# One stage of a fused image network: row sums from a ones column, a first key tile weighed in fp32, and one VectorE copy fewer

## The chip, the cores and the metric

The kernel runs on one core of a Trainium2 chip, in one launch. The metric is the device time of the whole launch in microseconds (us), the median of several runs. Only one of the kernel's stages is changed, and that stage takes about a sixth of the time.

## The reference, cut to what matters

The network has a windowed attention block, a gated convolution-like block, a plain self-attention, a pooling mixture of experts, a second attention with query, key and value weights, and a routed mixture of experts. It works on 32 images of 1024 tokens with 64 channels. The changed stage is the plain self-attention on layer-normed tokens:

```python
def _L2_attn_ref(seq):
    attn = jnp.einsum('blc,bmc->blm', seq, seq)
    attn = jax.nn.softmax(attn, axis=2)
    out = jnp.einsum('blm,bmc->blc', attn, seq)
    return out
...
t = t + _L2_attn_ref(_ln_t(t))        # t: 32 x 1024 x 64, fp32
```

Queries, keys and values are all the same normed tokens z. For one image the scores are z z^T (1024 x 1024), the weights are their softmax, and the result is the weights times z.

## The kernel before

The stage is `stage_attend`. Tokens stay on chip in fp32: 128 partitions by 8 tiles of 64 channels per image. Products keep fp32 accuracy by splitting each operand into a high f16 part and a low f16 rest. Since the score matrix is symmetric, a tile of 128 keys by 1024 queries that TensorE makes can be used as the stationary operand of the weighing directly, without a transpose.

An image has NT = 8 key tiles. For tile m the work is:

- **scores** (PE, L1259 and L1260): four matmuls of 512 columns into one of two PSUM buffers `ps_s`, from `xT` (high and low parts over each other) and from `xTb`, the same with its halves swapped by a DMA (L1140);
- **exp** (ACT, L1213): `ex` = exp(score - 55) in fp32, in a ring of 4, with the row sum taken by the instruction's accumulator into `rs`, which is a second instruction, ACTIVATION_READ_ACCUMULATOR;
- **high part** `exh` in f16: on ACT (L1219) for five tiles, on DVE (L1173) for tiles 1, 4 and 7;
- **low part** `exl` = `ex` - `exh` in f16 (DVE, L1166);
- **weighing** (PE, L1274 to L1277), LAG = 4 tiles later: for each of 8 query tiles three matmuls of 64 columns, high x high, high x low and low x high, summed in PSUM over all 8 key tiles. Each parity h of images has a bank of its own in `ps_o`.

After an image's last key tile DVE takes the reciprocal of the row sums (L1178), scales the result (L1181) and adds it to the tokens (L1184). These three are called the finish below.

The next images are prepared between the tiles by the slots `near` (next image) and `far` (next but one): at far 0 DVE sums and centres (L69, L74); at far 2 ACT squares (L80) and DVE reduces the squares (L85); at far 3 POOL makes the reciprocal root (L90, L92) and at far 4 the normed tokens `xn` (L98); at near 2 ACT takes their high part (`cut_high`, L106) and POOL the low part (`cut_low`, L113); at near 4 PE turns them (L126) into `ps_t` and DVE copies that to `xT` (L136), after which SP issues the two DMAs that fill `xTb`.

The order on each engine is written out by `stream` (L1047): for m = 0 to 7 it calls `step(m)` and the near and far slots. PE is given near and far after its step, as ACT and POOL are; DVE has `near_first`. In DVE's step m come the low part of tile m - 1, then its high part of tile m if it has one, then the finish, which was placed at step 4 of the next image. In PE's step m come the scores of tile m, then the weighing of the tile 4 back.

The waits that tie the engines: scores of tile m wait for exp of tile m - 2 (`exped`); exp of tile m waits for the low part of tile m - 4 (`low`); a weighing waits for its low part; scores of tile 0 wait for the DMAs (`swapped`). `cut_high` of the next image waits on ACT until the image before the current one has been weighed to its last tile (L1197), since it writes over that image's `hl`.

## Time and profile before

| what | value |
|---|---|
| median of 3 runs | 3016.01 us (3010.62 to 3026.71) |
| the profiled execution's own time | 3013.47 us |
| its span | 3011.3 us |
| mean granted TensorE clock | 0.923 of full speed |
| busy over the span: PE, DVE, ACT, POOL | 76%, 77%, 71%, 58% |

The changed stage lies between about 957 and 1489 us of the span. The shares above are means over all stages, so the stage has to be looked at by itself. An instruction's busy time and the time to the start of the next on its engine differ by up to 0.1 us, since instructions overlap at their ends; sums of a sequence therefore go by the distance between starts.

### The profile page before, as it was taken

What the parts mean: (1) busy time and instruction counts of PE and PEld (TensorE: products, weight loads), DVE (VectorE), ACT (ScalarE), POOL (GpSimd) and SP (SyncE); (2) the same over time, 40 slices, a digit from 0 to 9 for tenths busy, and PEclk for the clock granted to TensorE, in tenths of its full rate; (3) what the DMA queues carried; (4) which work ended last, traced back from release to release, by engine and by line L of the source; (5) the groups of instructions that cost most, each with busy time, mean ns of one, the idle gap of its engine ahead of it and who ended that gap; (6) DMA issues with size and microseconds to landing.
All of it is one profiled execution on the core that took longest, in us unless ns stands there. A gap on an engine that the chain in (4) does not pass through costs nothing. (4 is left out here: it accounts for less than half of the span.)

```text
span 3011.3 us, 86006 instructions
## 1 busy us (share of the span) xinstructions
PE 2282.4 (76%) x33244; PEld 1642.6 (55%) x33244; DVE 2327.7 (77%) x3714; ACT 2132.5 (71%) x3776; POOL 1742.0 (58%) x1370
## 2 busy tenths in 40 slices
PE   3777777778774888888644585888888888777777
PEld 1555555555552655555433473776777676545444
DVE  3677778777774999999867325888888887688897
ACT  2677777777773999999722112888888887777776
POOL 3577777777764333333266202998999898733331
PEclk9999999999996999999957556999999999899999
DMA  3211111111100000000000200000000000000101
GB/s 72 49 44 42 36 37 39 42 42 31 27 16 4 18 17 14 17 17 15 12 1 1 52 5 2 9 5 5 6 7 5 5 7 7 4 22 21 24 21 25
DMA packets 144669, 62.22 MB, mean 21 GB/s; under 512 B 118676, under 2 KB 127798, under 8 KB 144566
## 3 DMA queue, kind: packets, MB, share of 16 engines
q1 hardware_dynamic: 139565, 58.00, 9.0%
q10 hardware_dynamic: 4393, 2.77, 0.4%
q8 instruction: 73, 1.20, 0.2%
q14 instruction: 30, 0.25, 0.0%
q0 software_dynamic: 608, 0.01, 0.0%
HBM read 14.50 MB, written 8.39 MB: 8 GB/s over the span
## 5 line engine op out<-in xcount | busy, mean ns | idle before, releaser
L1813 POOL TENSOR_TENSOR a_prl<-a_pr,a_prh 128x1024 f16<-128x1024 f32 x256 | 544.9, 2142 | 47.8 <-ACT a_prh L1790 46.1
L1730 DVE TENSOR_REDUCE a_nmax<-a_ps_a 128x1 f16<-128x1024 f32 x256 | 312.2, 1219 | 34.0 <-PE a_ps_a L1852 32.1
L1166 DVE TENSOR_TENSOR a_exl<-a_ex,a_exh 128x1024 f16<-128x1024 f32 x256 | 319.4, 1269 | 8.4 <-ACT a_exh L1219 6.2
L1213 ACT ACTIVATE a_ex<-a_ps_s,a_shift 128x1024 f32<-128x1024 f32 x256 | 281.5, 1101 | 21.1 <-DVE a_exl L1166 12.8
L1790 ACT ACTIVATE a_prh<-a_pr 128x1024 f16<-128x1024 f32 x256 | 270.6, 1057 | 8.1
L1868 PE MATMUL a_ps_s<-a_qx,a_kh 128*128 128x128 f16 x2048 | 259.1, 220 | 2.7 <-issue 2.6
L1786 ACT ACTIVATE a_pr<-a_ps_s 128x1024 f32<-128x1024 f32 x256 | 259.5, 1014 | 0.0
L1870 PE MATMUL a_ps_s<-a_qm,a_kl 128*128 128x128 f16 x2048 | 259.2, 220 | 0.0
L2115 ACT ACTIVATE f_mixed_s<-f_ps_e,f_gates 128x64 f32<-128x64 f32 x1024 | 212.7, 426 | 40.1 <-PE f_ps_e L395 37.2
L113 POOL TENSOR_TENSOR a_w_hl<-a_w_xn,a_w_hl 128x512 f16<-128x512 f32 (+1 forms) x64 | 82.4, 1288 | 273.2 <-ACT a_w_hl L106 273.2
L1274 PEld LDWEIGHTS a_ps_o<-a_w_hl,a_exh 128*128 128x128 f16 x2048 | 181.9, 98 | 91.2 <-DVE a_exl L1166 66.2
L1274 PE MATMUL a_ps_o<-a_w_hl,a_exh 128*128 128x64 f16 x2048 | 207.1, 194 | 25.8 <-DVE a_exl L1166 25.8
L1868 PEld LDWEIGHTS a_ps_s<-a_qx,a_kh 128*128 128x128 f16 x2048 | 201.9, 99 | 34.7 <-issue 5.9
L1884 PE MATMUL a_ps_o<-a_vh,a_prh 128*128 128x65 f16 x2048 | 217.8, 196 | 3.3 <-POOL a_prl L1813 3.2
L1259 PE MATMUL a_ps_s<-a_w_xT 128*128 128x512 f16 x512 | 196.5, 384 | 31.0 <-DMA a_xTb<-a_w_xT 26.9
L1886 PE MATMUL a_ps_o<-a_vl,a_prh 128*128 128x65 f16 x2048 | 218.2, 193 | 0.0
L1870 PEld LDWEIGHTS a_ps_s<-a_qm,a_kl 128*128 128x128 f16 x2048 | 201.9, 99 | 29.5 <-issue 0.6
L1888 PE MATMUL a_ps_o<-a_vh,a_prl 128*128 128x65 f16 x2048 | 217.1, 194 | 0.0
L1852 PE MATMUL a_ps_a<-a_kh,a_qx 128*128 128x512 f16 x512 | 156.6, 388 | 68.0 <-DVE a_nmax L1730 63.5
L1277 PE MATMUL a_ps_o<-a_w_hl,a_exl 128*128 128x64 f16 x2048 | 206.2, 193 | 0.0
L1276 PE MATMUL a_ps_o<-a_w_hl,a_exh 128*128 128x64 f16 x2048 | 206.2, 193 | 0.0
L90 POOL TENSOR_TENSOR f_w_var<-f_w_ss,eps 128x8 f32<-128x8 f32 x64 | 12.8, 200 | 317.6 <-DVE f_w_ss L85 317.6
(344 smaller groups left out, 8526.7 us busy)
## 6 DMA issues: line engine op xcount, KB each, us to landing
tokens<-in_x_dram SPq DMA_DIRECT2D x32, 256.0 KB, 2.9
bl_qg<-bl_qk_high SPq DMA_DIRECT2D x128, 64.0 KB, 2.0
bl_km<-bl_qk_high SPq DMA_DIRECT2D x256, 32.0 KB, 2.0
a_xTb<-a_w_xT SPq DMA_DIRECT2D x64, 128.0 KB
out_dram<-tokens SPq DMA_DIRECT2D x32, 256.0 KB, 2.6
bl_qg<-bl_qk_low SPq DMA_DIRECT2D x64, 64.0 KB, 2.0
bl_km<-bl_qk_low SPq DMA_DIRECT2D x128, 32.0 KB, 2.0
a_qm<-a_qx SPq DMA_DIRECT2D x64, 64.0 KB, 2.0
```

What stands on the lines that cost most here:

```text
L1166: nc.vector.tensor_tensor(exl[:, at[2]], ex[:, r], exh[:, at[2]], ALU.subtract).then_inc(low, 1)
L1213: nc.scalar.activation(ex[:, r], ps_s[:, m % 2], ACT.Exp, bias=shift[:], accum_out=rs[at[1]][:, m:m + 1]).then_inc(exped, 1)
L1274: nc.tensor.matmul(out, e_high, z_high, start=(k == 0 and g == 0), stop=False, skip_group_check=True)
L1730: nc.vector.tensor_reduce(nmax[:, g:g + 1], ps_a[:], AX.X, ALU.max, negate=True).then_inc(maxed, 1)
L1786: nc.scalar.activation(pr[:, r], ps_s[:, m % 2], ACT.Exp).then_inc(exped, 1)
L1790: nc.scalar.activation(prh[:, r], pr[:, r], ACT.Copy).then_inc(high, 1)
L1813: nc.gpsimd.tensor_tensor(prl[:, r], pr[:, r], prh[:, r], ALU.subtract).then_inc(low, 1)
L1868: nc.tensor.matmul(out, kh[ha][:, keys], qx[ha][:, queries], start=True, stop=False, skip_group_check=True)
L1870: last = nc.tensor.matmul(out, kl[ha][:, keys], qm[ha][:, queries], start=False, stop=True, skip_group_check=True)
L1884: nc.tensor.matmul(out, high_j, vh[ha][:, j], start=(j == 0), stop=False, skip_group_check=True)
L1886: nc.tensor.matmul(out, high_j, vl[ha][:, j], start=False, stop=False, skip_group_check=True)
L1888: last = nc.tensor.matmul(out, low_j, vh[ha][:, j], start=False, stop=(j == NT - 1), skip_group_check=True)
```

## The change

- **Row sums.** The exp loses its accumulator output. `hl` is laid out as low, high, ones: the high part moves to columns 64 to 127 and column 128 holds 1.0. The two matmuls of a weighing that have the high part of z as moving operand take 65 columns, so the last column of each query tile's result is its row sum. The reciprocal reads that column from PSUM.
- **Three shared banks.** A result is now 8 x 65 = 520 columns, more than a bank's 512. The two parities lie in three banks: one from column 57 to 577, one from 959 to 1479. In the middle bank the first has its query tile 7, the second its query tile 0.
- **First key tile in fp32.** The exp of tile 0 goes to a buffer of its own, `whole`, and has no high and no low part: PE weighs it in fp32 against `xn` with a ones column (`xn1`), 8 matmuls of 65 columns in place of 24. Seven of them are issued in that tile's place, the eighth (the one in the shared bank) ahead of tile 1's weighing, after a wait for the scaling of the image before (`normed`).
- **High parts.** DVE takes those of tiles 2 and 5 in place of 1, 4 and 7. ACT has five as before.
- **Order on DVE.** The finish moves from the end of step 4 to the start of step 3, and now waits for the last weighing before the reciprocal.
- **POOL.** `xn` of the next image but one is made at far 6 in place of far 4, after a wait for the current image's tile 1 to be weighed, since PE reads `xn1`.

```diff
--- before.py
+++ after.py
@@ -100,17 +100,19 @@
-def cut_high(nc, ln, n1, w, x, n=C):
+def cut_high(nc, ln, n1, w, x, n=C, high=0):
     nc.scalar.wait_ge(ln["normed"], n1)
-    nc.scalar.activation(w["hl"][:, :, 0:n], x[:, :, 0:n], ACT.Identity).then_inc(ln["high"], 1)
-def cut_low(nc, ln, n1, w, x, engine=None, n=C):
+    nc.scalar.activation(w["hl"][:, :, high:high + n], x[:, :, 0:n], ACT.Identity).then_inc(ln["high"], 1)
+def cut_low(nc, ln, n1, w, x, engine=None, n=C, high=0):
...
     engine.wait_ge(ln["high"], n1)
-    engine.tensor_tensor(w["hl"][:, :, C:C + n], x[:, :, 0:n], w["hl"][:, :, 0:n], ALU.subtract).then_inc(ln["pair"], 1)
+    low = C - high
+    engine.tensor_tensor(w["hl"][:, :, low:low + n], x[:, :, 0:n], w["hl"][:, :, high:high + n],
+                         ALU.subtract).then_inc(ln["pair"], 1)
@@ -1080,25 +1082,29 @@
...
     RING, PARTS, LAG = 4, 8, 4
-    VECTOR_HIGH = (1, 4, 7)
+    WHOLE = 0
+    VECTOR_HIGH = (2, 5)
     with ExitStack() as ctx:
...
-        wk = [work_buffers(sb, f"w{h}") for h in range(2)]
+        wk = [work_buffers(sb, f"w{h}", ("sum", "ss", "var", "rstd", "xc", "sq", "hl", "xT")) for h in range(2)]
         xTb = [sb(f"xTb{h}", [P, TOK], F16) for h in range(2)]
...
         exl = sb("exl", [P, PARTS, TOK], F16)
-        rs = [sb(f"rs{h}", [P, NT], F32) for h in range(2)]
+        whole = sb("whole", [P, TOK], F32)
+        xn1 = [sb(f"xn1{h}", [P, NT, C + 1], F32) for h in range(2)]
+        for h in range(2):
+            wk[h]["xn"] = xn1[h][:, :, 0:C]
         rinv = [sb(f"rinv{h}", [P, NT], F32) for h in range(2)]
...
         ps_s = ctx.enter_context(nc.psum_tensor("a2_ps_s", [P, 2, TOK], F32))
-        ps_o = ctx.enter_context(nc.psum_tensor("a2_ps_o", [P, 2, 512], F32))
+        ps_o = ctx.enter_context(nc.psum_tensor("a2_ps_o", [P, 3 * 512], F32))
         ps_t = ctx.enter_context(nc.psum_tensor("a2_ps_t", [P, TOK], F16))
         ln = net.norms[0]
-        swapped, shift_set = (sem("a2_" + s) for s in ("swapped", "shift_set"))
+        swapped, shift_set, ones_set = (sem("a2_" + s) for s in ("swapped", "shift_set", "ones_set"))
@@ -1107,10 +1113,19 @@
...
+        OUTS = (512 - 7 * (C + 1), 1024 - (C + 1))
+        outs = [tiles(ps_o[:, at:at + NT * (C + 1)]) for at in OUTS]
+        SHARED, FRESH = (7, 0), ((0, 7), (0, 1))
         def count(at, lag=0):
...
             return NT * (2 * i + h) + m - lag + 1
+        def low_count(at):
+            i, h, m = at
+            return (NT - 1) * (2 * i + h) + m
@@ -1118,7 +1133,11 @@
...
                 return high_v, len(VECTOR_HIGH) * (2 * i + h) + before
-            return high_s, (NT - len(VECTOR_HIGH)) * (2 * i + h) + m + 1 - before
+            return high_s, (NT - 1 - len(VECTOR_HIGH)) * (2 * i + h) + m - before
+        def exps(at):
+            return whole[:] if at[2] == WHOLE else ex[:, at[2] % RING]
@@ -1143,6 +1162,9 @@
...
                 nc.vector.memset(shift[:], -SHIFT2).then_inc(shift_set, 1)
+                for h in range(2):
+                    nc.vector.memset(wk[h]["hl"][:, :, 2 * C:2 * C + 1], 1.0).then_inc(ones_set, 1)
+                    nc.vector.memset(xn1[h][:, :, C:C + 1], 1.0).then_inc(ones_set, 1)
@@ -1159,31 +1181,29 @@
...
                 def step(i, h, m):
+                    at = tile_at(i, h, m - LAG)
+                    if at and m == LAG - 1 or at and m == NT + LAG - 1:
+                        ia, ha, _ = at
+                        n = 2 * ia + ha
+                        dve.wait_ge(weighed, count(at))
+                        nc.vector.reciprocal(rinv[ha][:], outs[ha][:, :, C]).then_inc(inverted, 1)
+                        dve.wait_ge(inverted, n + 1)
+                        nc.vector.tensor_tensor(o[ha][:], outs[ha][:, :, 0:C], spread(rinv[ha][:], C),
+                                                ALU.mult).then_inc(normed, 1)
+                        dve.wait_ge(normed, n + 1)
+                        nc.vector.tensor_tensor(tv[:, ia, ha], tv[:, ia, ha], o[ha][:], ALU.add).then_inc(added, 1)
                     at = tile_at(i, h, m - 1)
-                    if at:
-                        r = at[2] % RING
+                    if at and at[2] != WHOLE:
                         dve.wait_ge(*high_count(at))
-                        nc.vector.tensor_tensor(exl[:, at[2]], ex[:, r], exh[:, at[2]], ALU.subtract).then_inc(low, 1)
+                        nc.vector.tensor_tensor(exl[:, at[2]], exps(at), exh[:, at[2]], ALU.subtract).then_inc(low, 1)
                     at = now(i, h, m)
                     if at and at[2] in VECTOR_HIGH:
-                        r = at[2] % RING
                         dve.wait_ge(exped, count(at))
...
                             dve.wait_ge(weighed, count(at, PARTS))
-                        nc.vector.tensor_copy(exh[:, at[2]], ex[:, r]).then_inc(high_v, 1)
-                    at = tile_at(i, h, m - LAG - 1)
-                    if at and at[2] == NT - 1:
-                        ia, ha, g = at
-                        n = 2 * ia + ha
-                        nc.vector.reciprocal(rinv[ha][:], rs[ha][:]).then_inc(inverted, 1)
-                        dve.wait_ge(inverted, n + 1)
-                        dve.wait_ge(weighed, count(at))
-                        nc.vector.tensor_tensor(o[ha][:], tiles(ps_o[:, ha]), spread(rinv[ha][:], C),
-                                                ALU.mult).then_inc(normed, 1)
-                        dve.wait_ge(normed, n + 1)
-                        nc.vector.tensor_tensor(tv[:, ia, ha], tv[:, ia, ha], o[ha][:], ALU.add).then_inc(added, 1)
-                stream(dve, step, near, far, LAG + 1, near_first=True)
+                        nc.vector.tensor_copy(exh[:, at[2]], exps(at)).then_inc(high_v, 1)
+                stream(dve, step, near, far, LAG, near_first=True)
                 dve.wait_ge(added, B)
@@ -1195,7 +1215,7 @@
...
                             act.wait_ge(weighed, NT * (2 * i + h - 1))
-                        cut_high(nc, ln, n + 1, w, w["xn"])
+                        cut_high(nc, ln, n + 1, w, w["xn"], high=C)
@@ -1204,19 +1224,18 @@
...
                     if at:
-                        r = at[2] % RING
                         act.wait_ge(scored, count(at))
-                        if past(at, RING):
-                            act.wait_ge(low, count(at, RING))
-                        if at[2] == 0 and past(at, 2 * NT):
-                            act.wait_ge(added, 2 * at[0] + at[1] - 1)
-                        nc.scalar.activation(ex[:, r], ps_s[:, m % 2], ACT.Exp, bias=shift[:],
-                                             accum_out=rs[at[1]][:, m:m + 1]).then_inc(exped, 1)
-                        if at[2] not in VECTOR_HIGH:
+                        if at[2] == WHOLE:
+                            if past(at, NT - 1):
+                                act.wait_ge(weighed, count(at, NT - 1))
+                        elif past(at, RING) and at[2] - RING != WHOLE:
+                            act.wait_ge(low, low_count(tile_at(at[0], at[1], at[2] - RING)))
+                        nc.scalar.activation(exps(at), ps_s[:, m % 2], ACT.Exp, bias=shift[:]).then_inc(exped, 1)
+                        if at[2] != WHOLE and at[2] not in VECTOR_HIGH:
                             act.wait_ge(exped, count(at))
...
                                 act.wait_ge(weighed, count(at, PARTS))
-                            nc.scalar.activation(exh[:, at[2]], ex[:, r], ACT.Copy).then_inc(high_s, 1)
+                            nc.scalar.activation(exh[:, at[2]], exps(at), ACT.Copy).then_inc(high_s, 1)
@@ -1225,13 +1244,15 @@
...
                     if k == 2:
-                        cut_low(nc, ln, n + 1, w, w["xn"], nc.gpsimd)
+                        cut_low(nc, ln, n + 1, w, w["xn"], nc.gpsimd, high=C)
...
                         norm_rstd(nc, ln, n + 1, w, net.nhalf[:], net.eps[:])
-                    if k == 4:
+                    if k == 6:
+                        if not isinstance(i, int) or 2 * i + h >= 2:
+                            pool.wait_ge(weighed, NT * (2 * i + h - 2) + WHOLE + 2)
                         norm_apply(nc, ln, n + 1, w, nc.gpsimd)
@@ -1262,22 +1283,38 @@
...
                         ia, ha, k = at
-                        pe.wait_ge(low, count(at))
-                        if k == 0 and past(at, 2 * NT):
-                            pe.wait_ge(added, 2 * ia + ha - 1)
-                        z_high, z_low = wk[ha]["hl"][:, k, 0:C], wk[ha]["hl"][:, k, C:2 * C]
+                        if k == WHOLE:
+                            pe.wait_ge(exped, count(at))
+                        else:
+                            pe.wait_ge(low, low_count(at))
+                        z_high, z_low = wk[ha]["hl"][:, k, C:2 * C + 1], wk[ha]["hl"][:, k, 0:C]
+                        def weigh_whole(g):
+                            return nc.tensor.matmul(outs[ha][:, g], whole[:, P * g:P * g + P], xn1[ha][:, WHOLE],
+                                                    start=g in FRESH[ha], stop=False, skip_group_check=True)
+                        if k == WHOLE:
+                            for g in range(NT):
+                                if g != SHARED[ha]:
+                                    ins = weigh_whole(g)
+                            ins.then_inc(weighed, 1)
+                            return
+                        if k == WHOLE + 1:
+                            if past(at, NT):
+                                pe.wait_ge(normed, 2 * ia + ha)
+                            weigh_whole(SHARED[ha])
                         for g in range(NT):
-                            out = ps_o[:, ha, C * g:C * g + C]
+                            out = outs[ha][:, g]
                             e_high = exh[:, k, P * g:P * g + P]
...
-                            nc.tensor.matmul(out, e_high, z_high, start=(k == 0 and g == 0), stop=False,
+                            nc.tensor.matmul(out, e_high, z_high, start=False, stop=False, skip_group_check=True)
+                            nc.tensor.matmul(out[:, 0:C], e_high, z_low, start=False, stop=False,
                                              skip_group_check=True)
-                            nc.tensor.matmul(out, e_high, z_low, start=False, stop=False, skip_group_check=True)
                             ins = nc.tensor.matmul(out, e_low, z_high, start=False, stop=(k == NT - 1),
...
+                pe.wait_ge(ones_set, 4)
                 stream(pe, step, near, nothing, LAG)
```

## Rows read from the trace of the kernel before

**Rows 1.** Windows view: us, busy of PE, PEld, DVE, ACT, POOL, clock, DMA share, GB/s.

```profile
1000.00:1460.00 460.00, 396.71 (x6606) 257.64 (x6603) 450.81 (x510) 434.35 (x657) 156.20 (x112) 1.00 0.07 16
```

**Rows 2.** Instruction groups, 1000 to 1460 us: count, busy us, mean ns, idle before, releaser.

```profile
L1166 DVE TENSOR_TENSOR a_exl<-a_ex,a_exh 128x1024 f16<-128x1024 f32 x229 | 285.4, 1268 | 2.0
...
L1173 DVE CAST a_exh<-a_ex 128x1024 f16<-128x1024 f32 x85 | 71.0, 835 | 0.0
...
L1213 ACT ACTIVATION_READ_ACCUMULATOR a_ex<-a_ps_s,a_shift 128x1 f32 x229 | 43.8, 191 | 0.0
```

**Rows 3.** Timeline of DVE, 1217 to 1227 us: start, us, engine, line, operation.

```profile
1217.58 0.69 DVE L1173 CAST a_exh<-a_ex 128x1024 f16<-128x1024 f32 x1
1218.31 2.06 DVE L1166 TENSOR_TENSOR a_exl<-a_ex,a_exh 128x1024 f16<-128x1024 f32 x1
1220.29 0.67 DVE L85 TENSOR_REDUCE a_w_ss<-a_w_sq 128x8 f32<-128x512 f32 x1
1220.89 1.21 DVE L1166 TENSOR_TENSOR a_exl<-a_ex,a_exh 128x1024 f16<-128x1024 f32 x1
1222.02 0.68 DVE L136 COPY a_w_xT<-a_ps_t 128x1024 f16<-128x1024 f16 x1
1222.62 1.21 DVE L1166 TENSOR_TENSOR a_exl<-a_ex,a_exh 128x1024 f16<-128x1024 f32 x1
...
1224.35 0.19 DVE L1178 RECIPROCAL a_rinv<-a_rs 128x8 f32<-128x8 f32 x1
1224.68 0.69 DVE L1181 TENSOR_TENSOR a_o<-a_ps_o,a_rinv 128x512 f32<-128x512 f32 x1
1225.52 0.69 DVE L1184 TENSOR_TENSOR tokens<-tokens,a_o 128x512 f32 x1
1226.13 1.22 DVE L1166 TENSOR_TENSOR a_exl<-a_ex,a_exh 128x1024 f16<-128x1024 f32 x1
```

**Rows 4.** Timeline of POOL, same stretch.

```profile
1217.59 1.70 POOL L113 TENSOR_TENSOR a_w_hl<-a_w_xn,a_w_hl 128x512 f16<-128x512 f32 x1 [8.43 <-ACT a_w_hl L106]
...
1222.23 1.64 POOL L92 TENSOR_TENSOR a_w_rstd<-a_w_var,nhalf 128x8 f32<-128x8 f32 x1
1223.95 1.38 POOL L98 TENSOR_TENSOR a_w_xn<-a_w_xc,a_w_rstd 128x512 f32<-128x512 f32 x1
```

**Rows 5.** Timeline of ACT, 1216 to 1223 us.

```profile
1216.90 0.61 ACT L106 ACTIVATE a_w_hl<-a_w_xn 128x512 f16<-128x512 f32 x1
1217.42 0.61 ACT L80 ACTIVATE a_w_sq<-a_w_xc 128x512 f32<-128x512 f32 x1
1217.94 1.09 ACT L1213 ACTIVATE a_ex<-a_ps_s,a_shift 128x1024 f32<-128x1024 f32 x1
...
1219.24 1.06 ACT L1219 ACTIVATE a_exh<-a_ex 128x1024 f16<-128x1024 f32 x1
1220.20 1.10 ACT L1213 ACTIVATE a_ex<-a_ps_s,a_shift 128x1024 f32<-128x1024 f32 x1
...
1221.29 1.10 ACT L1213 ACTIVATE a_ex<-a_ps_s,a_shift 128x1024 f32<-128x1024 f32 x1
```

**Rows 6.** Timeline of ACT in the later attention stage, 2117 to 2121 us.

```profile
2117.92 1.00 ACT L1786 ACTIVATE a_pr<-a_ps_s 128x1024 f32<-128x1024 f32 x1
2118.95 1.06 ACT L1790 ACTIVATE a_prh<-a_pr 128x1024 f16<-128x1024 f32 x1
```

**Rows 7.** Timeline of PE: first matmuls of two unstalled tiles.

```profile
1214.97 0.38 PE L1259 MATMUL a_ps_s<-a_w_xT 128*128 128x512 f16 x1
...
1216.53 0.38 PE L1259 MATMUL a_ps_s<-a_w_xT 128*128 128x512 f16 x1
```

**Rows 8.** Timeline of PE: first scores of an image.

```profile
1225.69 0.39 PE L1259 MATMUL a_ps_s<-a_w_xT 128*128 128x512 f16 x1 [0.93 <-DMA a_xTb<-a_w_xT]
```

**Rows 9.** Timeline of PE in the last stage: fp32 matmuls of 256 columns, then turns.

```profile
2970.31 3.72 PE L2176 MATMUL f_ps_x<-f_mixed_s,ident 128*128 128x256 f32 x16 [0.58 <-ACT f_mixed_s L2115]
2973.87 0.61 PE L126 MATMUL f_ps_t<-ident,f_w_hl 128*128 128x128 f16 x8
```

## The prediction

> **What bounds the kernel now.** The changed stage takes about 532 of 3011 us, so I read it alone. First the windows view of its middle: DVE is busy 450.8 of 460 us (98%), ACT 434.4, PE 396.7, at a granted clock of 1.00, the 2.4 GHz level [rows 1]. The groups view counts 229 low parts in that stretch, 28.6 images of 8, so an image takes 460 / 28.6 = 16.07 us, and DVE hardly ever waits [rows 2]. The timelines show how the other engines hang on it. DVE writes one operation behind the other [rows 3]. PE is held before an image's first scores by the swap of `xT`: the copy starts at 1222.02 and the scores at 1225.69, 3.67 us later, after 0.93 us of idleness [rows 3, 8]. DVE also pays for meeting POOL: the low part at 1218.31 lasts 2.06 us where its neighbours last 1.21, while POOL's `cut_low` runs from 1217.59 to 1219.29 [rows 3, 4]. From the means that is 8 x (1.268 - 1.22) = 0.4 us for low parts and 3 x (0.835 - 0.69) = 0.4 us for high parts, 0.8 us an image [rows 2, 3].
>
> **The change, part by part.**
>
> *DVE.* One low part goes: 1.13 us from start to start (1220.89 to 1222.02). One high part goes: 0.60 us (1223.75 to 1224.35 is the distance of one; its busy 0.69 less the overlap) [rows 2, 3]. DVE's sum is 16.07 - 1.13 - 0.60 = 14.34 us with the 0.8 us of meetings kept, 13.5 us with none. The reciprocal reads PSUM with a stride of 65 in place of SBUF: the trace has no such read, the nearest rows are 0.19 us for the SBUF form and 0.69 us for the scaling that reads 512 PSUM values [rows 3]; bounds 0 and +0.5, I take 0, since eight values are read.
>
> *ACT.* Eight accumulator reads go, 0.19 us each, 1.5 us busy, partly under the next instruction [rows 2]. What stays: exp to high part was 1.30 us (1217.94 to 1219.24), high part to exp 0.96, exp to exp 1.09, `cut_high` and square 0.52 each [rows 5]. Without accumulator the nearest pair is the PSUM copy and its f16 cast of the later stage, 1.03 us [rows 6]. Five tiles with a high part on ACT, as before: 5 x (1.03 + 0.96) + 3 x 1.0 + 1.04 = 14.0 us. Bounds: 13.7 (exp to exp 0.9, 1.09 less the read) and 15.6 (nothing shrinks: 5 x 2.26 + 3 x 1.09 + 1.04). I take 14.0, the row of the form that will run.
>
> *PE.* A full tile, scores and weighing, is 1.56 us (1214.97 to 1216.53) [rows 7]. Seven remain. Tile 0 keeps its scores, 0.87 of it, and swaps 24 f16 matmuls (0.70) for 8 fp32 ones. In the last stage 8 fp32 matmuls of 256 columns take 2973.87 - 2970.31 = 3.56 us, 0.445 each; by columns 65/256 of that is 0.113, so 0.90 in all [rows 9]. If the time did not shrink with the columns it were 3.56. I take 0.90, since the f16 steps do follow the columns. With the turns (at most 0.61 [rows 9]) PE sums to 7 x 1.56 + 0.87 + 0.90 + 0.6 = 13.3 us; upper bound 15.9. The 65th column adds 1/64 to two thirds of the weighings, under 0.1 us. The row sums and the third bank cost PE nothing else.
>
> *The moved finish and the waits.* The sums would allow 14.3, but the change closes a longer ring, and I take that as the bound. `cut_high` waits on ACT for the last weighing of the image before. Before, a high part of tile 2 stood ahead of it on ACT (0.96 us); tile 2 now belongs to DVE, so ACT reaches the wait earlier and stands in it, with the square and the exp of tile 3 queued behind. The square releases DVE's reduction of squares, which stands ahead of the finish, and the finish now stands ahead of the low part of tile 2 and of the next copy of `xT`, which starts the swap for the next image. Once round:
> - `xT` copy start to the next image's first scores: 3.67 [rows 3, 8];
> - four full tiles on PE until the image before is weighed, 4 x 1.56, and 0.2 until the last matmul is out: 6.44 [rows 7];
> - `cut_high` 0.52, then square and hand-over 0.66 [rows 5];
> - reduction 0.60 (1220.29 to 1220.89), finish 1226.13 - 1224.35 = 1.78, of which 0.2 is its meeting with POOL's `xn` (1223.95 to 1225.33), so 1.6 [rows 3, 4];
> - low part of tile 2: 1.13 [rows 3].
>
> Sum 14.62, I say 14.7 with the hand-overs. PE fits inside (13.3), and so does ACT (14.0 and a stand of about 0.7). The bounds of the ring are 14.3, if `cut_high` is not held, and 15.0.
>
> *The meetings with POOL.* In the ring DVE is idle when `cut_low` is asked for, and then comes the reduction, which I expect to pass beside POOL: the meeting is hidden. `xn` is asked for after POOL's 1.64 us root [rows 4], about 2.0 us after the reduction, in the low part of tile 2; it waits for that one's end, runs some 1.0 us beside the `xT` copy (0.60, reads PSUM), and the low part of tile 3 loses about 0.45. That lies outside the ring and inside DVE's slack (13.5 + 0.45 = 14.0). The wait for `weighed` on POOL is over by then. The `normed` wait on PE holds the weighing of tile 1 and, behind it, the scores of tile 6: scaling is over 1.1 us into the finish, PE gets there about 0.5 us later, so it costs nothing; if DVE were late by 1 us, PE would stand 0.5.
>
> Here the Trainium skill speaks, in "SBUF — State Buffer", section "Who interferes with whom": VectorE and GpSimd share a port pair, a VectorE instruction with two SBUF inputs contends with a GpSimd one that reads SBUF, and whoever starts first holds the pair for the whole instruction. By that rule the root would hold up the token addition of the finish. This trace disagrees for the root: the low part at 1222.62 lasts 1.21 us beside the root of 1222.23 to 1223.87 [rows 3, 4].
>
> *The total.* 16.07 - 14.7 = 1.37 us an image. Times 28.6 is 39; the 27 tiles outside the window, 3.4 images at the stage's ends with fewer preparations, I count at half, 2. So 41 to 42 us off the profiled execution's 3013.5 us. Its time is 2.5 us under the median of the runs, 3016.0; the same gain taken off the median gives **2974 us**.
>
> **The rivals.** With about 30 images' worth of gain:
> - *DVE stays the bound and meets POOL twice.* 13.5 + 0.84 (`cut_low`, the loss at 1218.31) + 0.45 to 1.0 (`xn`) = 15.2: 26 us gained, 2990. For it: such meetings happen in nearly every image now [rows 2 to 4]. Against: `cut_low` now follows exp 2 directly and falls in DVE's idle time.
> - *No ring.* If ACT is not held, or hand-overs run quicker than I count, ACT's or DVE's sum decides, 14.0: 62 us gained, 2954. For it: I have put the ring together from a schedule that the trace of before does not show. Against: each link has its row.
> - *Half of it comes.* The port is held by the root too, so that the addition waits about 1 us in the ring: 15.7, 11 us gained, 3005 (this is the rule above, from the page). Or ACT's exp does not shrink without its accumulator, so that the change does not do what it says there: 15.6, 3002. Or the fp32 matmuls cost 3.56: PE at 15.9, about the same. Against each stand the rows named above [rows 3, 4, 6, 9].
> - *Slower: both of POOL's operations fall into the ring.* If `xn` gets the port just ahead of the low part of tile 2, and `cut_low` just ahead of the high part of tile 2, each puts about 1.05 us into the ring: 14.7 + 2.1 = 16.8, 21 us lost, 3037. It decides from 1.37 us of extra in the ring. For it: a meeting of 1.0 us is in the trace. Against: both would have to hit at a certain 0.1 us in each image.
>
> **How the numbers follow.** Ring as worked out 0.42, two meetings 0.22, no ring 0.19, half of it 0.11, slower 0.06. The likeliest gives 2974. The range reaches to the no-ring case's 2954 and beyond it a little for ACT's lower bound (13.7), and up past the two meetings into the half case: 2948 to 3000. Over 0.5% faster means under 3001, and 0.5% is about what a measurement of this kernel can tell from no change. The first three cases and a part of the fourth lie under it: 0.86. Within 0.5%: 0.09. Slower by more: 0.05.
>
> **What would show each step.** In the stage's middle: low parts 7 to an image, no accumulator reads, exp about 1.02 us, exp to high part 1.03. `cut_high` on ACT with 0.5 to 0.9 us of idleness ahead of it, ended by PE's weighing; DVE idle ahead of the reduction, ended by the square; PE idle ahead of the first scores, ended by the swap. Image period 14.7; fp32 matmuls 0.113 us apart; low part of tile 3 about 1.6 us; clock still 1.00. If DVE is 98% busy, the second case holds; if ACT is, the third; if PE waits for `normed` or runs without idleness, I have PE wrong. A fall of the clock to 1.2 GHz inside the stage would overturn all of it.

## The result and the profile after

The changed kernel takes 2978.89 us (median of 3 runs, 2977.93 to 2982.43) where the kernel before takes 3016.01. The ratio is 0.988, 95% interval 0.9847 to 0.9913. The forecast was 2974 us, 42 us less; 37 us came.

Inside the profiled executions the gain is smaller. The changed stage, from its first `L69` to the next stage's first, took 534.4 us before and takes 506.3 after: 28.1 us less. The two spans, 3011.3 and 2980.6, differ by 30.7. The other 6 us of the medians' difference are within the scatter of the kernel before, whose medians in the comparisons below are 3024.9, 3013.2 and 3013.9. So I read every experiment by the length of the stage and by the period of an image, the mean distance of one `cut_high` from the next on ACT, 1000 to 1460 us: 16.17 before (the prediction has 16.07, from counting low parts in the window [rows 2]), 15.23 after, 14.7 forecast.

First the windows view of the stage's middle after, with the columns of [rows 1].

```profile
1000.00:1400.00 400.00, 384.72 (x5881) 281.07 (x5882) 360.65 (x421) 379.52 (x395) 103.97 (x104) 1.00 0.08 18
```

DVE is down from 98% to 90%, ACT is at 95%, PE up from 86% to 96%. The clock is 1.00 as before. DVE is no longer the bound, and two engines stand nearly level. The waits view, 1000 to 1430 us, in which each of the rows occurs once an image (columns: total us, times, longest):

```profile
POOL a_xn L98 <- PE a_ps_o L1313: 20.3, 28, 0.8
DVE a_w_ss L85 <- ACT a_w_sq L80: 19.9, 28, 0.8
DVE a_exl L1198 <- ACT a_exh L1238: 15.3, 28, 0.6
...
PE a_ps_s L1280 <- ACT a_ex L1233: 11.6, 29, 0.4
ACT a_w_hl L106 <- PE a_ps_o L1313: 10.8, 28, 0.4
```

There is no wait for the swap's DMA [rows 8] any more. PE now waits for ACT, and ACT for PE. The timeline of ACT shows one period, from one `cut_high` (`L106`) to the next:

```profile
1207.08 0.63 ACT L106 ACTIVATE a_w_hl<-a_xn 128x512 f16<-128x512 f32 x1 [0.43 <-PE a_ps_o L1313]
1207.62 0.61 ACT L80 ACTIVATE a_w_sq<-a_w_xc 128x512 f32<-128x512 f32 x1
1208.14 1.09 ACT L1233 ACTIVATE a_ex<-a_ps_s,a_shift 128x1024 f32<-128x1024 f32 x1
1209.34 1.06 ACT L1238 ACTIVATE a_exh<-a_ex 128x1024 f16<-128x1024 f32 x1
...
1217.74 1.09 ACT L1233 ACTIVATE a_whole<-a_ps_s,a_shift 128x1024 f32<-128x1024 f32 x1
1218.74 1.10 ACT L1233 ACTIVATE a_ex<-a_ps_s,a_shift 128x1024 f32<-128x1024 f32 x1
1219.87 1.06 ACT L1238 ACTIVATE a_exh<-a_ex 128x1024 f16<-128x1024 f32 x1
1220.84 1.09 ACT L1233 ACTIVATE a_ex<-a_ps_s,a_shift 128x1024 f32<-128x1024 f32 x1
1222.28 0.63 ACT L106 ACTIVATE a_w_hl<-a_xn 128x512 f16<-128x512 f32 x1 [0.35 <-PE a_ps_o L1313]
```

The exp is still 1.09 to 1.10 us without its accumulator. An exp is followed by its high part after 1.20 or 1.13 us (1208.14 to 1209.34, 1218.74 to 1219.87), by another exp after 1.00 (1217.74 to 1218.74). ACT runs without a gap from 1207.08 until exp 2 is through, and would reach the next `cut_high` at about 1221.85: 14.77 us of its own work. `cut_high` starts 0.43 later, at 1222.28 (0.35 by the row itself, which counts from the end of exp 2). The timeline of PE, of the same period:

```profile
1207.67 1.67 PE L1292 MATMUL a_ps_o<-a_xn,a_whole 128*128 128x65 f32 x14
1209.17 0.61 PE L128 MATMUL a_ps_t<-ident,a_w_hl 128*128 128x128 f16 x8
...
1215.34 0.39 PE L1280 MATMUL a_ps_s<-a_w_xT 128*128 128x512 f16 x1
...
1216.94 0.38 PE L1280 MATMUL a_ps_s<-a_w_xT 128*128 128x512 f16 x1
...
1218.89 0.39 PE L1280 MATMUL a_ps_s<-a_w_xT 128*128 128x512 f16 x1 [0.20 <-ACT a_whole L1233]
```

Seven fp32 matmuls (two records each) take 1.50 us from start to the next start, 0.214 each. The image's first scores, at 1215.34, have no idle time ahead of them: PE comes to them straight from the tile before. The scores of tile 2, at 1218.89, wait for the exp of tile 0, which empties their half of `ps_s`. And the timelines of DVE and, below it, of POOL:

```profile
1206.82 0.69 DVE L1204 CAST a_exh<-a_ex 128x1024 f16<-128x1024 f32 x1
1208.27 0.69 DVE L85 TENSOR_REDUCE a_w_ss<-a_w_sq 128x8 f32<-128x512 f32 x1 [0.75 <-ACT a_w_sq L80]
1208.87 0.20 DVE L1189 RECIPROCAL a_rinv<-a_ps_o 128x8 f32<-128x8 f32 x1
1209.10 0.69 DVE L1191 TENSOR_TENSOR a_o<-a_ps_o,a_rinv 128x512 f32<-128x512 f32 x1
1209.94 0.69 DVE L1194 TENSOR_TENSOR tokens<-tokens,a_o 128x512 f32 x1
1210.55 1.22 DVE L1198 TENSOR_TENSOR a_exl<-a_ex,a_exh 128x1024 f16<-128x1024 f32 x1
1211.68 0.68 DVE L138 COPY a_w_xT<-a_ps_t 128x1024 f16<-128x1024 f16 x1
1212.29 2.60 DVE L1198 TENSOR_TENSOR a_exl<-a_ex,a_exh 128x1024 f16<-128x1024 f32 x2
```

```profile
1207.79 1.12 POOL L114 TENSOR_TENSOR a_w_hl<-a_xn,a_w_hl 128x512 f16<-128x512 f32 x1 [10.33 <-ACT a_w_hl L106]
...
1209.31 1.64 POOL L92 TENSOR_TENSOR a_w_rstd<-a_w_var,nhalf 128x8 f32<-128x8 f32 x1
1211.63 1.04 POOL L98 TENSOR_TENSOR a_xn<-a_w_xc,a_w_rstd 128x512 f32<-128x512 f32 x1 [0.68 <-PE a_ps_o L1313]
```

DVE stands ahead of the reduction for the square, as forecast, and POOL's `cut_low` falls into that gap and beside the reduction: the 2.06 us low part beside a 1.70 us `cut_low` [rows 3, 4] has become 1.12 us on POOL and nothing on DVE.

### The profile page after: what moved, and what is told of

It reads as the page before. It is cut to its first block and busy times, and to the rows that moved or that the text cites. A ratio compares the mean times of both kernels' runs of the same rounds, so it can differ in the third digit from the quotient of the medians.

```text
span 2980.6 us, 85198 instructions
## 1 busy us (share of the span) xinstructions
PE 2303.2 (77%) x32988; PEld 1694.0 (57%) x32988; DVE 2260.9 (76%) x3654; ACT 2107.7 (71%) x3520; POOL 1694.9 (57%) x1370
## 5 line engine op out<-in xcount | busy, mean ns | idle before, releaser
L1198 DVE TENSOR_TENSOR a_exl<-a_ex,a_exh 128x1024 f16<-128x1024 f32 x224 | 275.6, 1260 | 29.6 <-ACT a_exh L1238 28.5
L1233 ACT ACTIVATE a_ex<-a_ps_s,a_shift 128x1024 f32<-128x1024 f32 x224 | 242.9, 1099 | 0.5 <-PE a_ps_s L1281 0.5
L114 POOL TENSOR_TENSOR a_w_hl<-a_xn,a_w_hl 128x512 f16<-128x512 f32 x32 | 36.0, 1124 | 318.4 <-ACT a_w_hl L106 318.4
L1281 PE MATMUL a_ps_s<-a_w_xT,a_xTb 128*128 128x512 f16 x512 | 195.0, 381 | 0.0
L1921 PEld LDWEIGHTS a_ps_o<-a_vh,a_prh 128*128 128x128 f16 x2048 | 191.8, 97 | 4.0 <-POOL a_prl L1850 2.6
L1925 PEld LDWEIGHTS a_ps_o<-a_vh,a_prl 128*128 128x128 f16 x2048 | 192.1, 97 | 0.0
L1923 PEld LDWEIGHTS a_ps_o<-a_vl,a_prh 128*128 128x128 f16 x2048 | 191.6, 99 | 0.0
```

The costliest lines, as they stand in the source:

```text
L1198: nc.vector.tensor_tensor(exl[:, at[2]], exps(at), exh[:, at[2]], ALU.subtract).then_inc(low, 1)
L1233: nc.scalar.activation(exps(at), ps_s[:, m % 2], ACT.Exp, bias=shift[:]).then_inc(exped, 1)
L1921: nc.tensor.matmul(out, high_j, vh[ha][:, j], start=(j == 0), stop=False, skip_group_check=True)
L1923: nc.tensor.matmul(out, high_j, vl[ha][:, j], start=False, stop=False, skip_group_check=True)
L1925: last = nc.tensor.matmul(out, low_j, vh[ha][:, j], start=False, stop=(j == NT - 1), skip_group_check=True)
```

## Experiments

"Changed" is the changed kernel run again. Each is timed beside the kernel before on its chip; three comparisons, set apart here by a rule. Stage and period are from the profiled executions.

| kernel | median us | ratio to before, 95% | stage us | period us |
|---|---|---|---|---|
| changed | 2983.17 | 0.9849 (0.9797-0.9901) | 507.0 | 15.23 |
| square first | 2970.44 | 0.9811 (0.9759-0.9863) | 501.3 | 15.05 |
| turn copy first | 2978.83 | 0.9840 (0.9787-0.9893) | 506.7 | 15.24 |
| three highs | 2972.57 | 0.9818 (0.9766-0.9871) | 495.9 | 14.90 |
| — | | | | |
| half the fp32 | 2982.27 | 0.9899 (0.9871-0.9927) | 506.9 | 15.25 |
| accumulators back | 2999.28 | 0.9958 (0.9943-0.9972) | 524.1 | 15.78 |
| before, no accumulators | 3004.71 | 0.9971 (0.9957-0.9985) | 536.5 | 16.32 |
| tile 0 in f16 | 3034.52 | 1.0074 (1.0045-1.0103) | 556.9 | 17.05 |
| — | | | | |
| square and three highs | 2996.71 | 0.9934 (0.9913-0.9955) | 520.9 | 15.74 |
| the same, half the fp32 | 2982.62 | 0.9903 (0.9873-0.9933) | 510.6 | 15.41 |
| before, two highs | 3046.79 | 1.0113 (1.0061-1.0164) | 552.5 | 16.67 |
| late finish | 3033.76 | 1.0064 (1.0039-1.0088) | 561.7 | 17.06 |

**The changed kernel again.**

> The changed kernel again, as the yardstick for the three beside it. All theories: an image every 15.24 us in the stage's middle, the stage 506 us from the first sum of tokens to the next stage's, the whole 35 to 38 us under the kernel before.

It repeats: the stage within 0.7 us, the period to 0.01.

**The copy of `xT` ahead of the low part of tile 2.** This cuts the forecast's ring alone.

```diff
-                    if k == 4:
+                    if k == 4 and isinstance(i, int) and (i, h) == (0, 0):
                         take_turned(...)          # its old place, now for the first image alone
...
+                    nx = tile_at(i, h, m + NT) if m == LAG - 1 else None
+                    if nx:
+                        take_turned(...)          # behind the token addition
                     at = tile_at(i, h, m - 1)     # low part of tile 2
```

> The changed kernel with DVE's copy of the turned tokens (L138) right behind the finish, ahead of the low part of tile 2 instead of behind it, so that the swap by DMA starts 1.13 us earlier. Ring through the swap: it shortens by 1.13 us, ACT's sum of 14.76 us is next, about 13 us off. Ring of ACT and PE: the swap has slack, nothing changes, within 3 us of the changed kernel. PE as the bound: nothing.

The period stays at 15.24 and the stage at 506.7. The swap starts 1.1 us sooner in the image and nothing follows there: it is not in what bounds the stage. The whole is 4.3 us under the changed kernel's, a little more than the 3 expected; the two kernels' times overlap (2975.3 to 2982.5 and 2980.6 to 2985.8).

**The square one step earlier on ACT.** `cut_high` then has an exp ahead of it rather than the square behind it.

```diff
-                    if k == 2:
+                    if k == 1:
                         norm_square(...)
```

> The changed kernel with ACT's square of the next image but one one slot earlier (far 1 in place of far 2), so that it stands ahead of cut_high and is not held by that one's wait. Ring through the swap (as forecast): reduction and finish no longer wait for cut_high and square, the ring shortens by over 1 us, and ACT's own sum of 14.76 us is next: 14.8 us an image, about 13 us off. Ring of ACT and PE (exp of tile 0, scores of tile 2, last weighing, cut_high): the stand of 0.43 us ahead of cut_high is filled by the square: 14.8 us, 13 us off as well. PE as the bound: nothing, 15.2 us.

The stage is 5.7 us shorter, as 0.18 us an image make it. The whole is 12.7 shorter; the other 7 lie outside the changed stage, and no run says why. ACT's stand ahead of `cut_high` is gone and ACT is at 385.08 of 400 us: the ring between PE and ACT was opened. The timelines of DVE and, below it, of POOL have the price of the shift: `xn` now starts 0.15 us behind the start of the low part of tile 3, and two low parts and `xn` all pay.

```profile
1207.66 3.20 DVE L1198 TENSOR_TENSOR a_exl<-a_ex,a_exh 128x1024 f16<-128x1024 f32 x2
```

```profile
1207.81 1.97 POOL L98 TENSOR_TENSOR a_xn<-a_w_xc,a_w_rstd 128x512 f32<-128x512 f32 x1 [1.22 <-PE a_ps_o L1313]
```

Two low parts take 3.20 us where two undisturbed ones take 2.36, and `xn` 1.97 where it took 1.04. DVE no longer has the slack for it, as a row of DVE and one of ACT show:

```profile
1203.04 0.69 DVE L1204 CAST a_exh<-a_ex 128x1024 f16<-128x1024 f32 x1 [0.65 <-ACT a_ex L1233]
```

```profile
1216.35 0.63 ACT L80 ACTIVATE a_w_sq<-a_w_xc 128x512 f32<-128x512 f32 x1 [0.17 <-DVE a_w_xc L74]
```

The square waits for DVE's centring in each of the 27 images between 1000 and 1400 us, and DVE waits for nothing but exp 2, which stands behind the square. From the high part of tile 2 (1203.04) DVE works without a gap to the centring (1215.62): 12.58; to the square 0.73, to exp 2 0.53, to the next high part 1.22, together 15.06, the period. ACT's own sum is still about 14.8; that the period is not 14.8, as expected, is this ring through DVE. That it binds is borne out two experiments further down, where one of its links grows and then another shrinks.

**A third high part on DVE.**

```diff
-    VECTOR_HIGH = (2, 5)
+    VECTOR_HIGH = (2, 5, 7)
```

> The changed kernel with three high parts on DVE (tiles 2, 5 and 7) and four on ACT. Ring of ACT and PE: ACT's part of it falls by a high part and the hand-over ahead of it, 1.1 us, until the next limit (the swap's ring without the wait for the exp of tile 0, 14.8 us, or PE's 14.1): 14.4 to 14.8 us, 12 to 24 us off. Ring through the swap: nothing, 15.2 us. If DVE were still the bound: 0.6 us an image more, 18 us slower.

The gain is 10.6 us whole and 11.1 in the stage, a little under the lower end. ACT lost a high part (0.97 us) and still the period fell only 0.33: ACT's stand ahead of `cut_high` grew to 0.62 to 0.70, and exp 1 now waits 0.3 to 0.5 for PE. ACT is at 362.19 of 400 us, DVE at 383.16, PE at 388.82 of 400: PE, with its one wait for ACT's exp, is the likely bound now; no run tests that.

**Half of the fp32 matmuls left out** (query tiles 3 to 6 get no weight from key tile 0).

```diff
-                                if g != SHARED[ha]:
+                                if g != SHARED[ha] and g not in (3, 4, 5, 6):
                                     ins = weigh_whole(g)
```

> The changed kernel with four of the eight fp32 matmuls of tile 0 left out (query tiles 3 to 6 lose that key tile's part). At 0.214 us each PE loses 0.86 us of work an image. Ring of ACT and PE by way of exp 0, scores 2, last weighing and cut_high: the fp32 matmuls are not in it, so nothing, 15.2 us an image and the same time within 3 us. PE as the bound: 0.86 us an image, 25 us off. The forecast's 0.113 us a matmul would have made it 0.45 us of work.

Nothing moves: PE falls from 384.72 to 368.92 of 400 us busy and the period stays at 15.25. The fp32 matmuls are not in the ring, and PE's own sum is not the bound, dear as they are.

**The accumulators back**, into a buffer that nobody reads.

```diff
+        rs = [sb(f"rs{h}", [P, NT], F32) for h in range(2)]
...
-                        nc.scalar.activation(exps(at), ps_s[:, m % 2], ACT.Exp, bias=shift[:]).then_inc(exped, 1)
+                        nc.scalar.activation(exps(at), ps_s[:, m % 2], ACT.Exp, bias=shift[:],
+                                             accum_out=rs[at[1]][:, m:m + 1]).then_inc(exped, 1)
```

> The changed kernel with the accumulator output back on every exp (written to a buffer that nobody reads). Ring of ACT and PE: the exps of tiles 3 to 7 lie in it, exp to high part goes from 1.17 back to about 1.27 us and exp to exp from 1.00 to 1.09, in sum 0.5 to 0.6 us: 15.8 us an image, 16 us slower. Were the swap or PE the bound: nothing.

17 us come back, 0.55 an image. The timeline of ACT shows the unit price:

```profile
1206.23 1.10 ACT L1234 ACTIVATE a_ex<-a_ps_s,a_shift 128x1024 f32<-128x1024 f32 x1
1207.22 0.19 ACT L1234 ACTIVATION_READ_ACCUMULATOR a_ex<-a_ps_s,a_shift 128x1 f32 x1
1207.32 1.11 ACT L1234 ACTIVATE a_ex<-a_ps_s,a_shift 128x1024 f32<-128x1024 f32 x1
```

From exp to exp it is 1.09 us with the read and 1.00 without. The read is 0.19 us busy but costs 0.09 to 0.10, since half of it lies under its neighbours.

**The kernel before, without accumulators** (its row sums are a constant 512).

```diff
+                    nc.vector.memset(rs[h][:], 512.0).then_inc(shift_set, 1)
...
-                        nc.scalar.activation(ex[:, r], ps_s[:, m % 2], ACT.Exp, bias=shift[:],
-                                             accum_out=rs[at[1]][:, m:m + 1]).then_inc(exped, 1)
+                        nc.scalar.activation(ex[:, r], ps_s[:, m % 2], ACT.Exp, bias=shift[:]).then_inc(exped, 1)
```

> The kernel before with only the accumulator outputs of the exps taken away (the row sums are then a constant, so the result is not scaled rightly). DVE as the bound of the kernel before: nothing, 16.1 us an image, within 5 us of it. ACT and DVE sharing the bound: up to 0.8 us an image, 23 us off.

The stage is 2 us longer, not shorter: in the profiled executions the accumulators cost nothing before the change, as is to be expected with DVE as the bound (391.69 of 400 us busy here). The whole time is 8.5 us lower, more than the 5 expected. The profile is of the slowest of this kernel's ten executions, 3012.66 us, so it can't show where the 8.5 come from; that stays open.

**Tile 0 weighed in f16 like the rest**, with its low part and three high parts back on DVE; the ones column, the shared banks and the early finish stay.

```diff
-    WHOLE = 0
-    VECTOR_HIGH = (2, 5)
+    WHOLE = None
+    VECTOR_HIGH = (1, 4, 7)
...
+                        order = [g for g in range(NT) if k or g != SHARED[ha]] + ([] if k else [SHARED[ha]])
```

> The changed kernel without the fp32 tile: tile 0 has a high and a low part like the others, and DVE takes high parts 1, 4 and 7 again, with the ones column, three banks and the early finish kept. DVE has 1.13 and 0.60 us more, PE 1.0 us less an image. Relief of DVE as what the gain is made of: 15.6 to 16.1 us an image, 12 to 25 us slower than the changed kernel. The ones column as what the gain is made of: 15.2 us or less.

It is slower than either theory had it: 17.05. The windows row, then from the timelines two of DVE's low parts and the two operations of POOL beside them:

```profile
1000.00:1400.00 400.00, 331.98 (x5478) 225.38 (x5476) 390.81 (x423) 342.07 (x353) 104.18 (x93) 0.97 0.07 16
```

```profile
1203.52 2.08 DVE L1198 TENSOR_TENSOR a_exl<-a_ex,a_exh 128x1024 f16<-128x1024 f32 x1
...
1214.70 2.02 DVE L1198 TENSOR_TENSOR a_exl<-a_ex,a_exh 128x1024 f16<-128x1024 f32 x1
```

```profile
1203.48 1.04 POOL L98 TENSOR_TENSOR a_xn<-a_w_xc,a_w_rstd 128x512 f32<-128x512 f32 x1 [1.30 <-PE a_ps_o L1303]
1214.12 1.52 POOL L114 TENSOR_TENSOR a_w_hl<-a_xn,a_w_hl 128x512 f16<-128x512 f32 x1 [9.59 <-ACT a_w_hl L106]
```

DVE is full again (98%) and pays for both of POOL's operations, 0.80 to 0.86 us each. PE stands up to 3.3 us an image for the scaling that frees the shared bank (65.9 us in 400). Relief of DVE is a condition of the whole gain; banks, ones column, early finish and the missing accumulators are a loss without it. The run takes away the fp32 tile and one moved high part together, so it does not tell the two apart.

**The finish at its old place**, behind the low part of tile 3 rather than ahead of that of tile 2.

```diff
-                    at = tile_at(i, h, m - LAG)
-                    if at and m == LAG - 1 or at and m == NT + LAG - 1:
+                    at = tile_at(i, h, m - LAG - 1)      # behind low and high part
+                    if at and at[2] == NT - 1:
...
-                stream(dve, step, near, far, LAG, near_first=True)
+                stream(dve, step, near, far, LAG + 1, near_first=True)
```

> The changed kernel with the finish at its old place on DVE, behind the low part of tile 3. The wait for the shared bank then holds the weighing of tile 1 about 2.3 us and the scores of tile 6 behind it, and exp 6 starts about 1.2 us late: 16.4 to 16.8 us an image, 33 to 45 us slower than the changed kernel. If the early finish were not needed: nothing.

17.06 us on the mean, where 16.4 to 16.8 was expected, and PE waits for the scaling (waits view, 1000 to 1400 us):

```profile
PE a_ps_o L1292 <- DVE a_o L1201: 48.6, 23, 2.2
```

The early finish is a condition of the shared banks. The forecast's "if DVE were late by 1 us, PE would stand 0.5" is this wait.

The mean hides two kinds of image. Most take 16.65 to 16.74 us, as expected. The five between 1000 and 1400 us that take 18.2 to 18.3 are the five in which the granted clock falls, each time behind such a stand of PE; two rows of the windows view, of the image that begins at 1076.29:

```profile
1080.00:1082.00 2.00, 0.00 (x0) 0.02 (x1) 1.83 (x3) 1.89 (x3) 1.06 (x1) 1.00 0.45 100
1083.00:1084.00 1.00, 1.00 (x16) 0.72 (x14) 1.00 (x2) 0.00 (x0) 0.16 (x1) 0.50 0.00 0
```

PE has nothing for 2 us at a clock of 1.00 and then works at 0.50, the 1.2 GHz level, until about 1086. That costs the image 1.6 us. PE stood 23 times and the clock fell five times, so a stand alone does not bring it.

**The kernel before with two high parts on DVE.**

```diff
-    VECTOR_HIGH = (1, 4, 7)
+    VECTOR_HIGH = (4, 7)
```

> The kernel before with one part of the change alone: high parts of tiles 4 and 7 on DVE, that of tile 1 on ACT. DVE loses 0.60 us an image, ACT, with its accumulators, gains 1.15 us on a sum of 15.3: 16.4 to 16.6 us, 5 to 15 us slower than the kernel before. If ACT had room (DVE the only bound): 15.5 us, 17 us faster.

The period, 16.67, is just above the 16.4 to 16.6 expected; the whole lost more than expected, 33 us, of which 18 lie in the stage. ACT is at 386.97 of 400 us. Moving a high part to ACT alone trades one bound for another. In the change it comes together with the accumulators and tile 0's high part gone; whether one of the two would be enough was not tested.

**Square first and three high parts together.**

```diff
-    VECTOR_HIGH = (2, 5)
+    VECTOR_HIGH = (2, 5, 7)
...
-                    if k == 2:
+                    if k == 1:
                         norm_square(...)
```

> The changed kernel with both: the square at far 1, and high parts 2, 5 and 7 on DVE. ACT's own sum falls to 13.7 us, so PE should bound: its work is 14.1 us an image, and its ring from exp 5 over the last weighing and cut_high back to exp 5 is 14.84 less the square's 0.52, 14.3 us. 14.3 to 14.5 us an image, 23 to 28 us under the changed kernel. If ACT were still the bound: 15.0. If the swap by DMA bound after all: 14.8.

A clear miss: 15.74 us instead of 14.3 to 14.5, worse than either alone. The waits view, 1000 to 1400 us, and ACT's timeline:

```profile
PE a_ps_s L1280 <- ACT a_ex L1233: 35.5, 25, 1.5
ACT a_w_sq L80 <- DVE a_w_xc L74: 32.9, 25, 1.4
```

```profile
1212.23 0.63 ACT L80 ACTIVATE a_w_sq<-a_w_xc 128x512 f32<-128x512 f32 x1 [1.23 <-DVE a_w_xc L74]
1212.77 1.10 ACT L1233 ACTIVATE a_ex<-a_ps_s,a_shift 128x1024 f32<-128x1024 f32 x1
```

DVE's timeline of the same image:

```profile
1202.82 3.20 DVE L1198 TENSOR_TENSOR a_exl<-a_ex,a_exh 128x1024 f16<-128x1024 f32 x2
...
1206.65 2.36 DVE L1198 TENSOR_TENSOR a_exl<-a_ex,a_exh 128x1024 f16<-128x1024 f32 x2
1208.93 0.69 DVE L1204 CAST a_exh<-a_ex 128x1024 f16<-128x1024 f32 x1
...
1211.51 0.69 DVE L74 SCALAR_TENSOR_TENSOR a_w_xc<-a_w_sum,tokens 128x512 f32<-128x512 f32 x1
...
1213.98 0.69 DVE L1204 CAST a_exh<-a_ex 128x1024 f16<-128x1024 f32 x1 [0.65 <-ACT a_ex L1233]
```

The third high part (1208.93) and `xn`'s meeting (the 3.20) push the centring to 1211.51. The square, moved ahead of exp 2, now waits 1.23 us for it; exp 2 and PE's scores of tile 4 wait behind the square; DVE waits 0.65 for exp 2. That is the ring through nearly all of DVE's work in which square first already stood, with a link more: its 15.06 and the third high part's 0.72 (1208.93 to the next low part at 1209.65) make 15.78. In the steady images of this run one `cut_high` follows the other after 15.79; the 15.74 of the table counts the stage's last ones too. Both edits had used the same slack on DVE.

**The same with half of the fp32 matmuls left out.**

```diff
-                                if g != SHARED[ha]:
+                                if g != SHARED[ha] and g not in (3, 4, 5, 6):
```

> The kernel of e8 with four of the eight fp32 matmuls left out (query tiles 3 to 6 lose that key tile's part), where e4 did the same with PE unhurried. PE as the bound of e8: 14.3 to 14.5 falls to 13.8 to 14.0, ACT's sum, 12 to 16 us under e8. DVE or the swap as the bound: nothing.

It gains 0.33 us an image (0.37 in the steady images, 15.79 to 15.42), where the changed kernel gained nothing from the same edit, but not as expected: PE has 361.11 of 400 us busy, no bound. `xn` waits for PE's weighing, is released earlier and meets less of DVE's low parts (2.82 us for the two instead of 3.20). Those 0.38 us are what the ring through DVE gains. So this run, too, was missed in size. From square first to here the period went up by one link of this ring and down by another, each time by that link's own change to about 0.01 us; a ring that does not bind would not do that.

## Why the prediction was right, and where it was not

**Sign, size and range held.** 2978.9 lies 5 us from the forecast and inside 2948 to 3000. DVE was the bound and was relieved; PE and ACT took over.

**The bounding ring was another one.** The forecast's ring went through the swap. Its links, read after: `xT` copy to first scores 3.66 (forecast 3.67), first scores to `cut_high` 6.94 (6.44), `cut_high` to reduction 1.19 (1.18), reduction 0.60, finish 1.68 (1.6), low part 1.13: 15.20 together. They add up to the period, as the links of any closed path do, so a sum that fits does not show that the path binds. The foretold idleness of PE ahead of the first scores is missing, and with the copy 1.1 us earlier the period stays. The step that failed is "*the change closes a longer ring, and I take that as the bound*": the ring is there, but has slack. It sits in the second link: four tiles of 1.59 and 0.2 make 6.56, and the other 0.38 of the 6.94 is PE's stand for the exp of tile 0. So the ring's own work is at most 14.8 us. What closes is between PE and ACT alone:
- exp of tile 0 on ACT (1217.74) frees the scores of tile 2 (1218.89) on PE;
- PE has two full tiles to do, 2 x 1.59 and 0.2, until the image before is weighed and `cut_high` may start at 1222.28: 4.54 us after that exp began, where ACT alone would need 4.11;
- `cut_high` and square 1.06;
- ACT without a gap from exp 3 to the next exp 0, 1208.14 to 1217.74: 9.60.

Sum 15.20. Square first, which opens this ring, gained; the third high part, which shortens it, gained; turn copy first and half the fp32, which lie outside, did not. These four are what shows it.

**Mis-sized terms.** "Exp to high part 1.03": 1.13 to 1.21, 5 x 0.14 = 0.7 us an image. The row I took, a PSUM copy of the later stage, is 1.00 us busy [rows 6]; the exp is 1.10 with and without its accumulator [rows 5]. Only the read's own 0.1 went, not the rival's nothing. ACT's sum is 14.77, not 14.0. "fp32 by columns 0.113": 0.214, so 8 cost 1.7, not 0.9. PE's tile is 1.59, not 1.56. PE sums to 7 x 1.59 + 0.86 + 1.70 + 0.45 = 14.1, forecast 13.3. So two engines stand within 1.1 us of the period, and each hand-over between them shows.

**Where the 28 us come from.** With accumulators back, 524.1: all the rest of the change gives 10 of the 28, the accumulators' 0.55 an image the other 17. The two are not shares that could be had singly. In the kernel before, taking the same accumulators away gave the profiled stage nothing, and without the relief of DVE the stage is 22 us longer than before.

**Right as forecast.** The stand ahead of `cut_high`, if a little shorter (0.35 to 0.43; I said 0.5 to 0.9), DVE's stand ahead of the reduction (0.75), `cut_low` passing at no cost, no wait for the scaling on PE, a reciprocal from PSUM at 0.20 us, the clock. `xn`'s meeting costs the low part of tile 3 about 0.25, not 0.45 (2.60 for two, 2.36 undisturbed).

**The rule on the port.** The root, 1.64 us on POOL from 1209.31, does not hold the token addition: 0.69 us at 1209.94. The Trainium skill ("SBUF — State Buffer", section "Who interferes with whom") says that an instruction of one of the two engines holds the shared port pair for its whole length; for the root this trace disagrees, as the one of before did [rows 3, 4]. The half case, of which this was a part, did not come by it. Where both sides are large (`xn`, `cut_low`), the meetings are there and cost DVE 0.84 to 0.85 us.

**Luck.** By the profiled executions 28 to 31 us came, and the forecast said 41 to 42. That the medians differ by 37 brings the forecast nearer than its working deserves.

**Open.** A version with both the earlier square and the third high part that also keeps centring early and `xn` clear of DVE's low parts was not tried. Nor was square first with `xn` kept off the low parts, which would test its ring directly. Either edit alone beats both kernels: 2970.4 and 2972.6 us in the same comparison as 2983.2.

## What to carry to other kernels

When one engine is relieved, add up every other engine's work an image and then look for the shortest loop of waits between the two that come next; a loop found on paper must be tested by moving one of its links, since its links add up to the period whether it binds or not. Slack on the relieved engine can be spent once: two edits that each gain by it may lose together. Take a term's duration from the very operation with its attribute removed, or hold both ends until there is one; a near relative was 0.14 us off, five times an image.

## What the runs showed of the hardware

- An fp32 matmul of 128x128 weights by 65 columns takes 0.214 us; one of 256 columns 0.445 [rows 9]. The time is not in proportion to the columns: a fourth of the columns takes half the time. An estimate from the two rows: some 0.14 us fixed.
- An accumulator on ACT does not lengthen the exp; its read, 0.19 us busy, costs 0.09 to 0.10 from start to start.
- The same pair of operations on DVE and POOL costs from nothing to 0.85 us by where the second one starts: `cut_low` beside an idle DVE 1.12 us, beside a low part 1.5 to 1.7; `xn` 1.04 or 1.97.
- In the two kernels in which PE stood 2 to 3 us at a time for DVE's scaling (tile 0 in f16, late finish), the granted clock fell to 0.50, the 1.2 GHz level, for some 3 to 7 us in five places each between 1000 and 1400 us, each time at or just behind such a stand; the mean there was 0.97 and 0.98. In all others it was 1.00. In the late finish each fall made its image 1.6 us longer. With tile 0 in f16 such an image was 1.2 to 2.2 us longer and the next one 2.0 shorter, so that little or nothing was lost.
